# Attention scores by key blocks and residue classes instead of a causal triangle

## The chip, the cores and the metric

The kernel runs on one core of one Trainium2 chip. The metric is the device time of one launch in microseconds (us). A core has five engines that run their own instruction streams side by side and meet through semaphores: PE (TensorE, the matmuls), DVE (VectorE), ACT (ScalarE), POOL (GpSimd) and SP (SyncE, which here only issues DMAs). Matmul results land in PSUM banks; everything else lives in SBUF or in DRAM.

## The reference

One transformer layer, 16 sequences of 512 tokens, width 256, 16 heads of 16, all inputs and outputs fp32:

```
OFFSETS = sorted(set(range(0, 33)) | {48, 64, 96, 128, 192, 256, 384})
scores = jnp.stack([jnp.einsum('bhnd,bhnd->bhn', q, _shift(k, delta, n)) for delta in OFFSETS], axis=-1) * scale
scores = scores + pos_bias.T[None, :, None, :]
alpha = jax.nn.softmax(scores, axis=-1)          # offsets that reach before token 0 are left out
for i, delta in enumerate(OFFSETS):
    out = out + alpha[..., i:i + 1] * _shift(v, delta, n)
gate = jax.nn.sigmoid(x @ Wgate + bgate)
x = layernorm(x + (flat * gate @ Wout + bout))
x = layernorm(x + moe(x))    # router, top 2 of 8 experts, capacity 1024, relu MLP 256 -> 1024 -> 256
```

So a query attends to 40 keys at most: those 0 to 32 tokens back, and seven at 48, 64, 96, 128, 192, 256 and 384 back, all multiples of 16. No other key counts.

## The kernel before

Three stages follow a setup: `attention` (attention, gate, first layer norm, router, scatter of tokens to experts), `experts` and `combine`. Only `setup` and `attention` are touched.

`attention` is a software pipeline over sequences. An iteration `it` has 16 slots, and in each slot every engine does a head part (one of the 16 heads of sequence `it`) and what the table `SLOTS_OF` lists: `proj` (q, k, v, gate projections of the next sequence), `maxp` (a bound for the softmax maximum of the next sequence from the allowed offsets: `near0` to `near3`, `far0`, `far1`, then `t`), `gate`, `outp` and `rout` (output projection, layer norm and router hidden layer of the previous one), `rank` (top 2, expert slots and scatter of the one before that). `split` and `feat` bring in the sequence after next. `AHEAD` says which sequence a stage works on; `LATER` by how many slots an engine comes after PE (1 if not listed). Iterations 2 to 13 are a hardware loop that holds two of them; the others are written out. Each engine runs its stream strictly in this order.

All matmuls are fp16 with a high and a low part, so that three products give nearly fp32. Heads are stacked in pairs on the partitions (e is 0 or 1, 64 partitions each): `qs`, `ks` hold high, low, high parts and in row 49 the negated maximum. For each head:

- PE (`scores`, L519): key-major scores of the causal triangle, four matmuls (512, 384, 256 and 128 queries), 1280 columns in three PSUM banks `st`.
- DVE (`biases`, L804): adds `score_bias`, which holds -1e30 for every offset that isn't allowed, while it moves the scores to `sc`.
- ACT (`weights`, L693, L694): exp twice over 1280 columns, to fp16 (`p16`) and to fp32 (`sc`).
- DVE or POOL (`split_weights`, L384; POOL has 8 of the 16 heads): the low part, fp32 less fp16.
- PE (`values`, L533, L535): 20 matmuls with 128x128 weights into `opv`; ACT (L687) copies pairs of heads to `ob`.

The maximum is found with short matmuls already: near offsets in blocks of 32 queries (L598), far ones by classes of tokens modulo 16 (L615), since all far offsets are multiples of 16. In `rank`, DVE works out the slots (L926 to L947), POOL issues 8 indirect DMAs (L1002) from `y16`, and ACT's next write of `y16` (L761, in `outp` part `y`) waits until they have landed; L887 on DVE makes its low part. `setup` writes `bias_vec`, 128 shifted copies of each head's bias vector, to DRAM, and attention reads it back as `score_bias`.

## Time and profile before

| | us |
|---|---|
| median of 3 runs | 2248.94 (2247.68 to 2251.49) |
| the profiled execution, its own time | 2257.1 |
| its span, first to last instruction | 2255.3 |
| setup, to the first load of attention | 78.85 |
| one iteration of the loop (projection to projection) | 102.0 on average |
| share of the span: DVE, PE, ACT, POOL busy | 71%, 68%, 59%, 40% |

A start in the rows below is in us from the span's start. A PE matmul's duration includes its passage through the array, so a run of short ones is read from start to start. "<-issue" marks idle time in which the engine waited for nothing that the profile shows.

### The profile page before, as it was taken

How to read it: one execution, taken by the hardware profiler on the slowest of the kernel's cores; microseconds unless marked ns; L12 is line 12 of the kernel's file. 1: busy time of each engine (PE TensorE's matmuls, PEld its weight loads, DVE VectorE, ACT ScalarE, POOL GpSimd, SP SyncE). 2: the span in 40 equal slices, each digit the busy share in tenths (PEclk: the TensorE clock that was granted, in tenths of full speed). 3: DMA queues.
4: the chain of work that ended last, by engine and by line, in shares of the span. 5: the costliest groups of instructions: out<-in, count | busy, mean ns of one | idle time of the engine just before them, and what ended most of it. 6: DMA issues, size and time to landing. Idle time of an engine off the chain costs nothing. (4 is left out here: it accounts for less than half of the span.)

```text
span 2255.3 us, 53211 instructions
## 1 busy us (share of the span) xinstructions
PE 1532.9 (68%) x21152; PEld 910.7 (40%) x21152; DVE 1603.1 (71%) x3026; ACT 1333.3 (59%) x1736; POOL 897.9 (40%) x681
## 2 busy tenths in 40 slices
PE   0257778676858677676868586776764499999910
PEld 0134434343434334343434343443432256676710
DVE  4048898887979797977879797979886255555422
ACT  1236776675848576665758585766764366566423
POOL 1223444535454444445354444445353113233242
PEclk9965686776767586776667685867656699999965
DMA  7934331313132230312131321302000334444256
GB/s 108 186 94 141 67 58 50 55 43 62 40 59 51 48 58 32 58 38 52 32 53 47 54 48 34 58 24 48 22 21 12 95 95 85 106 105 88 31 121 196
DMA packets 145705, 150.88 MB, mean 67 GB/s; under 512 B 26287, under 2 KB 134847, under 8 KB 145296
## 3 DMA queue, kind: packets, MB, share of 16 engines
q1 hardware_dynamic: 130112, 132.47, 25.2%
q0 software_dynamic: 15360, 15.10, 4.2%
q8 instruction: 171, 2.80, 0.5%
q14 instruction: 62, 0.51, 0.1%
HBM read 84.70 MB, written 73.70 MB: 70 GB/s over the span
## 5 line engine op out<-in xcount | busy, mean ns | idle before, releaser
L384 POOL TENSOR_TENSOR p<-sc,p 128x1280 f16<-128x1280 f32 x128 | 336.4, 2628 | 536.7 <-ACT sc L694 536.7
L693 ACT ACTIVATE p<-sc 128x1280 f16<-128x1280 f32 x256 | 328.8, 1284 | 360.5 <-PE opv L535 167.6
L804 DVE TENSOR_TENSOR sc<-st,score_bias 128x512 f32<-128x512 f32 (+3 forms) x1024 | 427.5, 478 | 67.4 <-PE st L519 47.1
L694 ACT ACTIVATE sc<-sc 128x1280 f32<-128x1280 f32 x256 | 325.8, 1273 | 0.0
L519 PE MATMUL st<-qs,ks 49*128 49x512 f16 (+3 forms) x1024 | 267.6, 378 | 50.1 <-DVE sc L804 37.2
L384 DVE TENSOR_TENSOR p<-sc,p 128x1280 f16<-128x1280 f32 x128 | 216.0, 1688 | 14.1 <-ACT sc L694 13.2
L533 PE MATMUL opv<-vs,p 128*128 128x33 f16 x2560 | 176.1, 184 | 68.6 <-issue 30.1
L504 PE MATMUL gp<-featT,wr 128*128 128x512 f16 x768 | 204.0, 423 | 1.5 <-ACT featT L708 1.1
L533 PEld LDWEIGHTS opv<-vs,p 128*128 128x128 f16 x2560 | 154.5, 100 | 109.6 <-issue 85.1
L1253 POOL DMA_INDIRECT xln<-y,place x64 | 105.3, 1645 | 220.2 <-DVE y L1395 201.6
L862 DVE TENSOR_REDUCE m_near<-gp 128x8 f16<-128x512 f32 x128 | 82.6, 684 | 148.9 <-remote 92.7
L535 PE MATMUL opv<-vs,p 128*128 128x17 f16 x2560 | 171.8, 175 | 17.1 <-issue 17.1
L1291 PE MATMUL up<-rowsT,w 128*128 128x512 f16 x768 | 173.2, 386 | 9.6 <-DVE w L1368 5.3
L1002 POOL DMA_INDIRECT disp<-y,sidx x128 | 135.2, 1056 | 104.2 <-issue 68.6
L1305 PE MATMUL dn<-w,h 128*128 128x256 f16 x1536 | 170.1, 273 | 0.0
L497 PE MATMUL gp<-ident,x 128*128 128x128 f16 x512 | 53.7, 272 | 170.1 <-ACT x L715 83.9
L1352 ACT ACTIVATE h<-up,b 128x512 f16<-128x512 f32 x128 | 88.1, 688 | 131.1 <-PE up L1291 71.8
L708 ACT COPY featT<-gp 128x1024 f16<-128x1024 f16 x96 | 96.7, 1045 | 111.9 <-PE gp L497 111.6
L535 PEld LDWEIGHTS opv<-vs,p 128*128 128x128 f16 x2560 | 150.7, 100 | 30.0 <-issue 22.2
L1305 PEld LDWEIGHTS dn<-w,h 128*128 128x128 f16 x1536 | 149.7, 98 | 17.3
L519 PEld LDWEIGHTS st<-qs,ks 49*128 49x128 f16 x1024 | 90.2, 108 | 164.5 <-DVE sc L804 79.6
L1407 DVE TENSOR_TENSOR h<-h 128x512 f16<-128x512 f32 x128 | 88.7, 693 | 69.6 <-ACT h L1353 69.6
(158 smaller groups left out, 2956.1 us busy)
## 6 DMA issues: line engine op xcount, KB each, us to landing
qk_dram<-qk SPq DMA_DIRECT2D x64, 256.0 KB, 2.5
qs<-qk_dram SPq DMA_DIRECT2D x96, 128.0 KB, 4.5
ks<-qk_dram SPq DMA_DIRECT2D x96, 128.0 KB, 7.7
disp<-y SPq DMA_DIRECT2D x8, 1040.0 KB, 14.3
rows<-disp SPq DMA_DIRECT2D x16, 520.0 KB, 3.7
xin<-in_L_attn_x SPq DMA_DIRECT2D x16, 512.0 KB, 3.9
xres<-in_L_attn_x SPq DMA_DIRECT2D x16, 512.0 KB
xln<-y SPq DMA_DIRECT2D x16, 512.0 KB, 2.9
```

The lines of the kernel that those rows point to most:

```text
L384: engine.tensor_tensor(p16[:, h % 2, 1, :], sc[:, h % 2, :], p16[:, h % 2, 0, :], ALU.subtract).then_inc(plo_pool if h in POOL_HEADS else ...
L504: last = nc.tensor.matmul(dst, lhs(a, c), rhs(b, c), start=(k == 0), stop=(k == len(todo) - 1))
L519: last = nc.tensor.matmul(st[bank][:, at:at + w], ks[n.par][rows, p, P * j:P * (j + 1)], qs[n.par][rows, p, P * j:N], start=True, stop=True)
L533: nc.tensor.matmul(opv[:, h % 2, i, :], p16[:, h % 2, 0, c:c + P], vs[n.par][:, j, h, :], start=(j == 0), stop=False, skip_group_check=True)
L535: last = nc.tensor.matmul(opv[:, h % 2, i, 0:HD + 1], p16[:, h % 2, 1, c:c + P], vs[n.par][:, j, h, 0:HD + 1], start=False, stop=(j == i), ...
L693: nc.scalar.activation(p16[:, h % 2, 0, :], sc[:, h % 2, :], ACT.Exp)
L694: nc.scalar.activation(sc[:, h % 2, :], sc[:, h % 2, :], ACT.Exp).then_inc(exp_ready, 1)
L804: last = nc.vector.tensor_tensor(sc[:, h % 2, COL[j]:COL[j] + w], st[bank][:, at:at + w], score_bias[:, e, p, 0:w], ALU.add)
L1002: nc.gpsimd.indirect_dma_start(out=disp[:, :], out_offset=bass.IndirectOffsetOnAxis(ap=sidx[:, t, k:k + 1], axis=0), in_=y16[:, t, :].bitc ...
L1253: nc.gpsimd.indirect_dma_start(out=xln[:, :], out_offset=bass.IndirectOffsetOnAxis(ap=place[:, gr, t:t + 1], axis=0), in_=y[:, gr, t, :], ...
L1291: last = nc.tensor.matmul(up[h % 4][:, :], w1[e.par][:, a, c, P * h:P * (h + 1)], rowsT[:, gr, b, c, :], start=(k == 0), stop=(k == 5))
L1305: last = nc.tensor.matmul(dn[u][:, D * (t % 2):D * (t % 2 + 1)], h16[:, gr, a, h, P * t:P * (t + 1)], w2[e.par][:, b, h, :], start=(k == 0 ...
```

## The change

Scores are computed only where offsets can be allowed, in six units ("pairs", since each fills one PSUM bank for each e) for all 16 heads of a sequence, in place of 16 heads. Pairs 0 and 1 are far: tokens of one class modulo 16 against each other, 32x32. Pairs 2 to 5 are near: 64 keys by 32 queries. The bias is added on PE by matmuls of a 0/1 matrix (`sel`) with high and low fp16 parts of the bias (L561, L583), so DVE's pass is gone and ACT reads PSUM. DVE splits bank e = 0 of each pair and POOL bank e = 1. Values need v rearranged in both ways: `vs` goes to DRAM (`v_dram`) and comes back as `v_far` and `v_near`. Far results are evacuated by ACT to `o_far`, written to `o_dram` and read back in token order (`o_back`); DVE adds them to the near results (`merge`, L910). `SLOTS_OF` is arranged anew, and `setup` has no `bias_vec`. A loop iteration has 2496 matmuls instead of 1162: 512 for scores and 1152 for values that are 32 or 64 wide, where 64 and 320 full-width ones stood; 48 more add the bias to the scores; `maxp` keeps its 512 short ones.

```diff
-COL = {0: 0, 1: 512, 3: 896, 2: 1024}
-SCW = 1280
-GP_BANKS, ST_BANKS = 3, 4
+FAR_PAIRS, NEAR_PAIRS = 2, TILES
+GP_BANKS, ST_BANKS = 3, 3
...
+    5: [("outp", "t"), ("rank", "c")],
+    6: [("outp", "w"), ("maxp", "near0"), ("rank", "s0"), ("rank", "s1")],
+    7: [("rank", "s2"), ("rank", "s3"), ("outp", "y"), ("maxp", "near1")], 8: [("maxp", "near2"), ("maxp", "near3")],
+    9: [("maxp", "far0")], 10: [("maxp", "far1"), ("rout", "t"), ("split", "x")],
...
+SCORES_AT = [-1, 0, 4, 7, 10, 12]
+EXP_AT = [0, 1, 5, 8, 11, 13]
+SPLIT_AT = [1, 2, 6, 9, 12, 14]
+VALUES_AT = [2, 4, 7, 10, 13, 15]
+EVAC_AT = [3, 5, 8, 11, 14, 16]
...
+        def split_weights(eng, engine, n, k, e, is_split):
+            eng.wait_ge(exp_ready, n.at(2 * UNIT_PAIRS, 2 * k + e + 1))
+            b = 2 * (k % 2) + e
+            engine.tensor_tensor(p16[:, b, 1, :], p32[:, b, :], p16[:, b, 0, :], ALU.subtract).then_inc(is_split, 1)
...
+                if h == 6:
+                    wait(sp, o_in, n.at(16))
+                    sp.wait_ge(far_out, n.at(FAR_PAIRS, FAR_PAIRS))
+                    for r4 in range(4):
...
+                        sync.dma_start(dst, src).then_inc(o_stored, 16)
+                    wait(sp, merged, n.at(TILES))
+                    sp.wait_ge(o_stored, n.at(64, 64))
+                    sync.dma_start(o_back[:, :, :, :].rearrange("p t h c -> p t (h c)"), o_dram.rearrange("(t p) c -> p t c", p=P)).then_inc(o_in, 16)
...
+            def scores(n, k):
+                if k == 0:
+                    alone.wait_ge(m_in[n.par], n.half(32, 32))
+                wait(alone, exp_ready, n.at(2 * UNIT_PAIRS, 2 * k + 2 - ST_BANKS))
...
+                            for w in range(4):
+                                for e in range(2):
+                                    last = nc.tensor.matmul(banks[e][BLOCK * w:BLOCK * (w + 1), c:c + BLOCK], key[rows[e], 2 * w + z, r:N:FAR_STEP],
+                                                            q[rows[e], 2 * w + z, r:N:FAR_STEP], start=False, stop=(z == 1 and r8 == 7 and w == 3),
...
+                    for b in range(4):
+                        quad = slice(BLOCK * b, BLOCK * (b + 1))
+                        for z in range(4):
+                            for e in range(2):
+                                c = P * z + BLOCK * b
+                                for j, (a, cols) in enumerate(terms3):
+                                    for u in range(2):
+                                        at = (2 * z + e) * OW
+                                        last = nc.tensor.matmul(o[u][quad, at:at + cols.stop - cols.start],
+                                                                p16[halves[u], 2 * (k % 2) + e, a, c:c + BLOCK],
+                                                                v_near[halves[u], 4 * i + b, 2 * z + e, cols],
...
+            def weights(n, k):
+                wait(act, pv_done, n.at(UNIT_PAIRS, k - 1))
+                for e in range(2):
+                    act.wait_ge(st_full[e], n.at(UNIT_PAIRS, k + 1))
+                    bank, b = st[(2 * k + e) % ST_BANKS], 2 * (k % 2) + e
+                    nc.scalar.activation(p16[:, b, 0, :], bank[:, :], ACT.Exp)
+                    nc.scalar.activation(p32[:, b, :], bank[:, :], ACT.Exp).then_inc(exp_ready, 1)
...
-                for vec, copies, src in ((bias_vec, P, vec_b), (near_vec, 32, vec_n), (far_vec, 32, vec_f)):
-                    sp.dma_start(vec, src.unsqueeze(1).to_broadcast([H, copies, vec.shape[2]])).then_inc(stored, 16)
```

DVE before, in the loop, from the residual add of `outp` on: the add and the layer norm's statistics, then a head's bias adds and split, two maximum reductions, another head, and only after `far0`'s reductions the low part of `y16`, which waits for ACT's L761.

```order
L876 SCALAR_TENSOR_TENSOR y<-gp,xres 128x512 [waits xres_ready,gp_full1]
...
L804 TENSOR_TENSOR sc<-st,score_bias 128x512 [waits st_full2,plo_dve]
L804 TENSOR_TENSOR sc<-st,score_bias 128x384 [waits st_full3]
L804 TENSOR_TENSOR sc<-st,score_bias 128x128
...
L866 TENSOR_REDUCE m_far<-gp 128x2x8 [waits gp_full1]
L353 REGISTER_ALU
L866 TENSOR_REDUCE m_far<-gp 128x2x8 [waits gp_full2]
L887 TENSOR_TENSOR y<-y 128x4x256 [waits yh_ready]
```

DVE after, the same stretch: `near0`'s reductions, the first merge, then the low part of `y16` (L992), and behind it the reductions of `near1`, a split, and those of `near2`.

```order
L981 SCALAR_TENSOR_TENSOR y<-gp,xres 128x512 [waits xres_ready,gp_full1]
...
L910 TENSOR_TENSOR ob<-o,o_back 128x136 [waits pv_done]
L910 TENSOR_TENSOR ob<-o,o_back 128x136
L992 TENSOR_TENSOR y<-y 128x4x256 [waits yh_ready]
L368 REGISTER_ALU
L967 TENSOR_REDUCE m_near<-gp 128x8 [waits gp_full1]
L967 TENSOR_REDUCE m_near<-gp 128x8 [waits gp_full2]
L393 REGISTER_ALU
L395 TENSOR_TENSOR p<-p 128x512 [waits exp_ready]
L967 TENSOR_REDUCE m_near<-gp 128x8 [waits gp_full0]
```

What moved: L992 now stands ahead of the reductions that free `gp` banks for `near2`, `near3` and `far0`.

PE after, from the last slot to the first of the next iteration: scores of pair 0, the transposes of `feat`, and scores of pair 1, which need a bank that the exps of pair 0 must have left.

```order
L568 MATMUL st<-qs,ks 32x32 x64
L645 REGISTER_ALU
L130 REGISTER_ALU [waits xh_ready]
L537 MATMUL gp<-ident,x 128x128 [waits gp_drained1]
L537 MATMUL gp<-ident,x 128x128 x7
L537 MATMUL gp<-ident,x 128x128 [waits gp_drained2,xl_ready]
L537 MATMUL gp<-ident,x 128x128 x7
L95 REGISTER_ALU
L561 MATMUL st<-sel,far_bias 128x256 [waits exp_ready]
```

Before, the transposes stood ahead of a head's values and there were four `st` banks.

## Rows read from the trace of the kernel before

**Rows 1.** Windows (stretch, us; PE, PEld, DVE, ACT, POOL busy; granted clock; DMA): iterations 0, 1, 6.

```profile
144.35:218.55 74.20, 51.51 (x961) 28.50 (x961) 53.18 (x96) 50.32 (x59) 30.73 (x17) 0.62 0.53 155
218.55:307.65 89.10, 68.92 (x1085) 39.07 (x1085) 76.84 (x120) 67.52 (x86) 39.07 (x23) 0.73 0.24 49
812.92:917.13 104.21, 74.00 (x1163) 41.81 (x1163) 89.85 (x160) 68.95 (x87) 48.07 (x31) 0.72 0.23 49
```

**Rows 2.** The page, part 5: what the softmax costs off PE.

```profile
L384 POOL TENSOR_TENSOR p<-sc,p 128x1280 f16<-128x1280 f32 x128 | 336.4, 2628 | 536.7 <-ACT sc L694 536.7
L693 ACT ACTIVATE p<-sc 128x1280 f16<-128x1280 f32 x256 | 328.8, 1284 | 360.5 <-PE opv L535 167.6
L804 DVE TENSOR_TENSOR sc<-st,score_bias 128x512 f32<-128x512 f32 (+3 forms) x1024 | 427.5, 478 | 67.4 <-PE st L519 47.1
...
L384 DVE TENSOR_TENSOR p<-sc,p 128x1280 f16<-128x1280 f32 x128 | 216.0, 1688 | 14.1 <-ACT sc L694 13.2
```

**Rows 3.** Groups by form, 800 to 1000 us: two 512-wide reads of PSUM.

```profile
L777 ACT ACTIVATE hid<-gp,br 128x512 f16<-128x512 f32 x15 | 10.9, 728 | 5.5 <-PE gp L504 5.5
L862 DVE TENSOR_REDUCE m_near<-gp 128x8 f16<-128x512 f32 x16 | 10.3, 683 | 18.3 <-remote 16.6 <-PE gp L598 1.6
```

**Rows 4.** Timeline of DVE, POOL and ACT in iteration 6: rank, scatter, layer norm.

```profile
847.66 2.15 DVE L926 TENSOR_SCALAR rdiff<-rexp 128x4 f32<-128x4 f32 x1
853.53 0.16 DVE L947 TENSOR_SCALAR token_id<-token_id 128x4 f32<-128x4 f32 x1
854.71 1.11 POOL L1002 DMA_INDIRECT disp<-y,sidx  x1 [2.62 <-issue]
864.14 0.98 POOL L1002 DMA_INDIRECT disp<-y,sidx  x1 [0.30 <-issue]
870.39 1.28 DVE L876 SCALAR_TENSOR_TENSOR y<-gp,xres 128x512 f32<-128x512 f32 x2
873.92 0.25 POOL L980 TENSOR_SCALAR veps<-mv 128x4 f32<-128x4 f32 x1 [8.80 <-DVE mv L884]
875.83 0.91 POOL L985 TENSOR_TENSOR nmr<-nmr,rstd 128x4 f32<-128x4 f32 x1 [0.18 <-POOL rstd L983]
880.12 1.04 ACT L761 CAST y<-y 128x1024 f16<-128x1024 f32 x1
881.19 1.23 DVE L887 TENSOR_TENSOR y<-y 128x1024 f16<-128x1024 f32 x1 [0.49 <-ACT y L761]
```

**Rows 5.** Timeline of PE: value matmuls, then short ones in one run.

```profile
820.19 0.18 PE L533 MATMUL opv<-vs,p 128*128 128x33 f16 x1 [0.67 <-ACT ob L687]
...
820.24 0.18 PE L533 MATMUL opv<-vs,p 128*128 128x33 f16 x1
...
877.97 1.41 PE L615 MATMUL gp<-ks,qs 16*32 16x32 f16 x128
```

**Rows 6.** PE's instruction packets, MB: whole page, then 1118 to 1122 us; idle times.

```profile
q8 instruction: 171, 2.80, 0.5%
...
q8 instruction: 2, 0.03, 2.9%
...
881.14 0.19 PE L535 MATMUL opv<-vs,p 128*128 128x17 f16 x1 [1.14 <-issue]
1120.95 0.20 PE L533 MATMUL opv<-vs,p 128*128 128x33 f16 x1 [3.65 <-issue]
```

**Rows 7.** Timeline of PE: projections of q and k in iteration 14.

```profile
1532.17 5.28 PE L504 MATMUL gp<-featT,wqk 128*128 128x512 f16 x12 [1.18 <-issue]
1538.60 2.76 PE L504 MATMUL gp<-featT,wqk 128*128 128x512 f16 x12
```

**Rows 8.** Setup: a DMA's KB and us to landing; DVE's last work; PE's first `near0`.

```profile
bias_vec<-og SPq DMA_DIRECT2D x1, 5120.0 KB, 55.0
...
41.19 3.47 DVE L1137 MEMSET ks<- 32x4096 f16 x1 [0.89 <-issue]
...
116.15 0.61 PE L591 MATMUL gp<-near_mask,sel_first 64*128 64x512 f16 x2 [14.17 <-issue]
```

More of the change, by code:

```diff
@@ L187, in run_iterations, with pair_at @@
         one(Batch(None, c))
-def head_at(it, k):
-    n = it.shift(k // H)
-    return (n, k % H) if n.in_range() else None
+def pair_at(it, slot, table):
+    for k, at in enumerate(table):
+        if at % H == slot and it.shift(-(at // H)).in_range():
+            return it.shift(-(at // H)), k
 def tail(rows, dt):
@@ L523, in values @@
[L523 to L536 removed]
+            alone = Apart(pe, pe_passed)
@@ L537, in values @@
                 last.then_inc(pv_done, 1)
             def head(it, k):
[L541 to L543 removed]
+                for what, table in ((values, VALUES_AT), (scores, SCORES_AT)):
+                    if pair_at(it, k, table):
+                        what(*pair_at(it, k, table))
             def feat(n, part):
```

381 lines of the change are left out of this document (221 added, 160 removed), and 9 rows, old and new, of the table SLOTS_OF.

## The prediction

> **What bounds the kernel now.** I read the windows of single iterations first, then the timelines of DVE, POOL, ACT and PE inside one of them. In a loop iteration of 104.2 us DVE works for 89.9, PE for 74.0, ACT for 69.0 and POOL for 48.1 [rows 1]. DVE is within 14 us of full, so it sets the pace, and what feeds it is the softmax: the bias adds (64 a sequence by 478 ns, 30.6 us) and half of the splits (8 by 1.69 us, 13.5 us) [rows 2]. ACT has 32 exps of 1.28 us (41 us), POOL 8 splits of 2.63 us (21 us) [rows 2]. The change takes aim at the right engine; the question is what is late next.
>
> **DVE, ACT and POOL after.** The bias adds are gone. Six pairs leave 6 splits of 512 columns each for DVE and POOL: 512/1280 of 1.69 us is 0.68 us, 4.1 us a sequence, and of 2.63 us 1.05 us, 6.3 us [rows 2]. ACT has 24 exps of 512 columns from PSUM at 0.73 us, 17.5 us [rows 3]. The four merges are two short PSUM reads each, below 0.68 us [rows 3], so 5 us at most; they replace the sum of high and low parts. DVE falls from 90 to about 50 us, ACT to 45, POOL to 33. None of them can bound an iteration any more by its work; by its order, yes (below).
>
> **PE after.** 384 matmuls go, 1712 come. How dear is a short one? Rows of before bound it from both sides. 128 matmuls of 32x32 ran in 1.41 us with 0.24 us of passage in it: 9 ns each [rows 5]. Value matmuls with full-width weights start at 820.19 and, two further, at 820.24: some 26 ns each [rows 5]. The new value matmuls are 32 wide like the cheap ones, but 24 to 48 in a row go to the same 32 columns of the array with only two row halves in turn, where the cheap ones cycle through four column groups. I take 20 ns for values (a pair's 192: 3.8 us) and 10 to 15 ns for scores with their bias matmuls (far pair 2.1 us, near pair 1.2 us).
>
> Instruction supply sets a second floor. PE's queue brought 2.80 MB in 171 packets [rows 6], 16 KB or 128 matmuls with their weight loads. After the loop's branch PE idled 3.65 us and two packets fell into 4 us; after the burst of 128 short ones it idled 1.14 us for no other reason shown [rows 6]. I read this as about 3.1 us a packet once the one in hand is used up: 24 ns a matmul in long runs. An iteration now needs 20 packets, 62 us of its 104, so supply is no bound on average, only inside dense runs, where 20 ns with a packet in hand costs the same. The Trainium skill (Runtime: NRT & Kernel Launch, Instruction fetch mechanics) describes such a fetch, in 16 KiB blocks of 256 instructions, and gives PE an instruction memory of 128 KiB. By that size eight blocks would lie ready and dense runs would not wait, which is rival B below; the idle times in the rows speak against it.
>
> **An iteration after, as a round.** I follow what must be waited for, from the end of pair 2's scores (slot 4).
>
> First leg, off PE. ACT: four exps (2.9 us) [rows 3], two copies of far results and the small exp that `rank` needs (1.0 us, guessed from the small rows of 0.16). DVE: the rank chain, 847.66 to 853.69, 6.0 us [rows 4]. DVE: residual and statistics, 870.39 to 873.92, 3.5 us [rows 4]. POOL: 873.92 to 876.74, 2.8 us [rows 4]. POOL: eight indirect DMAs, 854.71 to 865.12, 10.4 us [rows 4]; they now stand behind that layer norm step. Landing of the last: 2 us (between nothing and the 3 us of other small writes). Then ACT's L869, which waits for it, 1.04 us, and DVE's L992, which waits for L869, 1.23 us [rows 4], and one reduction of `near1`, 0.68 us [rows 3], which frees the bank for `near2`. Ten handoffs at 0.15 us add 1.5. Sum 33.1 us. PE has until then only `outp` t and w, `near0`, values of pair 2, scores of pair 3, `near1`: about 18 us. So PE waits some 14 us here. Before, L761 came at 880.12, 15 us after the last indirect DMA [rows 4], and nobody waited. Behind L869 on ACT stand the exps of pair 3; behind L992 on DVE the reductions and the split of pair 3.
>
> Second leg, PE's own order. `near2` and `near3` at the pace of DVE 4; `far0`, values 3, scores 4, `far1` 10; `rout` and `maxp` transposes with ACT's copy 4; four router steps, two of q, k, two of v and gate. Such a step (12 matmuls of 512) takes 2.6 us at the high granted clock and 5.1 at the low one [rows 7]; I take 2.9, eight are 23.5. Scores 5 and values 4: 5. Values 5, scores 0, `feat`: 7.7. Then a new wait: scores 1 need the first exp pair of pair 0, behind ACT's two `feat` copies, 2.9 us; scores 1, 2.0. Values 0 and 1, the router logits (64 at 26 ns), scores 2: 10.5. Sum 69.6 us. Both legs: 102.7 us. Before, 12 iterations took 1532.17 - 307.65 = 1224.5, 102.0 each [rows 1, 7]. **So the loop gains nothing:** DVE's 40 us are given back to PE and to the scatter chain.
>
> DMA is added too (v out and back twice, far results out and back). v comes back during the projections, which hides it. The far results' trip (store and load, some 8 us) starts at slot 6 and the first merge is wanted on DVE some 14 us after slot 4; it is in time if the stack loads of `qs`, `ks` don't hold it, and even if late by 10 us it ends before L869 does.
>
> **What is surely gained.** Setup waits for `bias_vec`: 5120 KB that take 55 us to land, until attention starts at 78.85 (the table) [rows 8]. Without it the end of setup is DVE's last memset, 44.7 us, plus 3 for more small copies and start-up: -31 us. The first `near0` (116.15) comes a further 3 us sooner, since 4 MB of `score_bias` no longer crowd its loads [rows 8]. Iteration 0 has no scatter, layer norm or router: 74.2 us with DVE at 53 and ACT at 50 [rows 1], by PE's order about 67, -7. Iteration 1 has no scatter: 89.1 to 85, -4. The last iterations without projections: -8. Sum -53.
>
> **Sum.** Loop: 12 x (102.7 - 102.0) = +8. Span 2255.3 - 53 + 8 = 2210. The profiled execution took 2257.1, the median of the runs is 8.2 lower; so 2202 in runs. The legs use durations measured beside a DVE and a POOL that are far busier than they will be; I shorten the round by 0.6 us for that and say **2195 us** (a loop iteration of 102.1).
>
> **Rivals.**
> A, the forecast: iteration 98 to 106.5, 2146 to 2248. Chance 0.45.
> B, short matmuls cost 9 to 12 ns everywhere and supply holds. Values fall from 3.8 to 2 us, five of them on the round: -9 us, and -1.5 from scores. Iteration 92, 2195 - 12 x 10 = 2075. For it: 9 ns in a row. Against: the idle in [rows 6]. Chance 0.23.
> C, slower: each short matmul costs what a full-width one does, 26 to 27 ns [rows 5], and more where supply waits. Values 5.0 us (+6 on the round), scores and `maxp` on the round +6: iteration 114 to 115, 2195 + 12 x 12.5 = 2345. It decides from iteration 106.6 on. For it: same tile in a row, and during the indirect DMAs before, PE is fed slowly too. The Trainium skill (TensorEngine Tiling (Array Packing), Instruction Overhead) puts about 60 cycles on each matmul however small, 25 ns at 2.4 GHz by estimate; the 9 ns of the row contradict it for tiles that alternate, not for these. Chance 0.23.
> D, the far results or v come late, and merges hold DVE and PE beyond the scatter chain: +4 us an iteration, 2245. Chance 0.09.
>
> **Range and chances.** From B's end to short of C's: 2065 to 2330. No change is what a measurement can't tell, within 0.2% (4.5 us). Faster: nearly all of A and B and half of D, 0.68; same 0.05; slower 0.27.
>
> **What would show it.** DVE near 50 us of an iteration; PE busy above 80. PE idle before `near2` some 10 us or more, put down to DVE's reductions, with L869 right after the last indirect DMA's landing. PE idle about 3 us before scores 1 on ACT. Value matmuls 20 ns from start to start, 192 in 3.8 us, with idle by issue in the runs. Setup's end near 48 us. Wrong if values run at 10 ns (then 2075), if PE idles by issue for more than 10 us an iteration beyond today's (then above 2250), or if merges wait for `o_back`.

## The result, and the profile after

The changed kernel takes 2491.99 us (median of 4, 2485.14 to 2502.4), the kernel before 2250.22 beside it: ratio 1.108, 95% interval 1.103 to 1.113. The forecast was 2195 with a range to 2330. The change costs 242 us where I expected a gain of 54.

The page of the changed kernel, engine shares and PE's instruction packets:

```profile
span 2483.5 us, 94541 instructions
PE 1632.6 (66%) x42496; PEld 1076.5 (43%) x42496; DVE 961.5 (39%) x1989; ACT 908.2 (37%) x1544; POOL 648.6 (26%) x654
q8 instruction: 338, 5.54, 0.9%
```

Its windows (columns as in [rows 1]): iterations 0 and 1, then eight loop iterations, from the router logits of one sequence to those eight later.

```profile
116.21:216.37 100.16, 54.44 (x2323) 37.99 (x2315) 24.29 (x36) 23.93 (x47) 16.30 (x15) 0.59 0.54 147
216.37:322.89 106.52, 75.81 (x2427) 49.09 (x2419) 41.99 (x57) 41.72 (x73) 24.24 (x22) 0.68 0.35 73
693.40:1649.50 956.10, 643.93 (x19970) 419.08 (x19969) 363.84 (x712) 331.10 (x593) 251.17 (x233) 0.67 0.32 69
```

The same eight iterations before:

```profile
622.70:1445.20 822.50, 588.53 (x9300) 333.59 (x9300) 694.32 (x1250) 544.06 (x688) 379.45 (x249) 0.70 0.22 47
```

An iteration now takes 119.5 us instead of 102.8. DVE is down from 86.8 to 45.5 us an iteration, ACT from 68.0 to 41.4, POOL from 47.4 to 31.4: what the change aims at is there in full. PE is now the only engine that works more, so I account for its time. Its waits in that stretch (us in total, times, longest), the larger ones:

```profile
PE o L632 <- issue: 68.4, 51, 4.1
PE st L588 <- issue: 46.1, 71, 1.6
PE o L618 <- issue: 45.7, 12, 7.9
PE gp L689 <- DVE m_near L967: 25.4, 16, 2.8
PE st L568 <- issue: 21.7, 16, 2.0
PE gp L537 <- issue: 20.5, 5, 4.8
PE st L561 <- issue: 19.7, 4, 5.6
```

With the small ones, "issue" is 240 us, 30.0 an iteration; before it was 58, 7.3 an iteration. The table below, made the same way for each kernel (windows and PE's waits over eight iterations), is what all that follows is read from. The last three columns add up to the iteration.

| kernel, beside a before of | whole, us | iteration | PE busy | idle by issue | PE waits for others |
|---|---|---|---|---|---|
| before, 2250 | 2250 | 102.8 | 73.6 | 7.3 | 21.6 |
| changed, 2250 | 2492 | 119.5 | 80.5 | 30.0 | 8.9 |
| changed again (c1), 2251 | 2504 | 121.0 | 81.2 | 31.5 | 8.1 |
| changed again (c0), 2147 | 2504 | 121.1 | 79.2 | 24.9 | 16.9 |

So PE is busy 7 us longer, stands 23 us longer for its own instructions, and waits 13 us less for others: +17. Of the 7 us 1.6 are the projection and router steps, whose 512 column matmuls are the same ones but ran at a lower granted clock (0.67 in these iterations against 0.70). In two of the six sets of measurements the kernel before took 2250 us, in the other four 2145 to 2147, by the chip they fell on; the changed kernel took 2492 to 2504 on both kinds of chip. On the first kind idle by issue is larger, on the second the wait for `m_near`. I compare times within one kind; e8, e9 and e10 ran on the first, all other edits on the second.

**What an issue stall is.** PE's timeline of the changed kernel, the values of one pair (192 matmuls) with a stall inside, then an undisturbed pair:

```profile
951.85 1.94 PE L632 MATMUL o<-v_near,p 64*32 64x17 f16 x160 [0.53 <-issue]
956.38 0.60 PE L632 MATMUL o<-v_near,p 64*32 64x17 f16 x32 [2.60 <-issue]
```

```profile
778.12 2.34 PE L632 MATMUL o<-v_near,p 64*32 64x17 f16 x192
```

Undisturbed, 192 take 2.34 us with 0.17 of passage: 11 ns each, near the 9 ns of [rows 5] and not the 20 I took. With a stall inside, the same work takes 5.1 us.

A packet holds 256 instructions, 128 matmuls with their weight loads, so the undisturbed pair has a packet boundary in it too. It cost nothing: a packet had started at 776.66, during the 24 long matmuls before this run, and was there in time. Counting PE's instructions from the loop's branch on shows where the stalls lie. In c0's eight iterations 59 stalls over 0.9 us begin at one and the same place modulo 256, at 7.4 of the 20.5 packet boundaries of an iteration, and PE goes on 1.2 to 1.9 us after a packet has landed. They add up to 20.1 us an iteration; in the first profile they are 56 and 19.2 us. At the other boundaries PE stands for less or not at all. It never gets far ahead: in c0 the packet that started at 1062.15 was the last one for 483 instructions, not quite two packets' worth, and then PE stood.

**How long it lasts depends on the DMA engines.** c0, values of pair 1, and the DMA queues during the stall (packets, MB, share of 16 engines), first part and last part:

```profile
1070.46 1.63 PE L618 MATMUL o<-v_far,p 64*32 64x34 f16 x153
1079.89 0.66 PE L618 MATMUL o<-v_far,p 64*32 64x32 f16 x39 [7.80 <-issue]
```

```profile
q1 hardware_dynamic: 718, 0.65, 115.8%
...
q1 hardware_dynamic: 620, 0.61, 95.7%
q8 instruction: 1, 0.02, 3.4%
```

From 1072.0 to 1076.9 no instruction packet moves, while data fills the engines (the stack loads, and `v_dram<-vs`, which came with the change); PE's packet moves only after 1076.9. Now a stall of c0 with no data on the DMA engines; the only traffic from 1020.9 to 1023.2, which is the packet itself; and the window of the long stall (the last two columns are DMA's share and GB/s):

```profile
1023.25 0.23 PE L632 MATMUL o<-v_near,p 64*32 64x16 f16 x4 [2.06 <-issue]
```

```profile
q8 instruction: 1, 0.02, 3.0%
```

```profile
1072.00:1079.80 7.80, 0.09 (x11) 0.00 (x0) 0.00 (x0) 0.52 (x2) 1.06 (x2) 0.80 1.11 164
```

With no data to pass, a boundary in a dense run costs 2.06 us, with full engines 7.80.

**The off-PE leg**, DVE in c0, then in the run with y stored later (e1, second run):

```profile
967.90 1.25 DVE L967 TENSOR_REDUCE m_near<-gp 128x8 f16<-128x512 f32 x2
978.93 0.50 DVE L910 TENSOR_TENSOR ob<-o,o_back 128x136 f32<-128x136 f32 x2 [9.78 <-DMA o_back<-o_dram]
984.83 1.23 DVE L992 TENSOR_TENSOR y<-y 128x1024 f16<-128x1024 f32 x1 [5.39 <-ACT y L869]
985.97 1.28 DVE L967 TENSOR_REDUCE m_near<-gp 128x8 f16<-128x512 f32 x2
```

```profile
924.82 1.25 DVE L967 TENSOR_REDUCE m_near<-gp 128x8 f16<-128x512 f32 x2
934.83 0.51 DVE L910 TENSOR_TENSOR ob<-o,o_back 128x136 f32<-128x136 f32 x2 [8.76 <-DMA o_back<-o_dram]
935.25 1.28 DVE L967 TENSOR_REDUCE m_near<-gp 128x8 f16<-128x512 f32 x2
```

The reduction that PE needs for `near2` stands behind two waits: the far results' return, then the scatter through L869 and L992. With y later only the first is left. What PE does meanwhile, c0 (from the transposes behind pair 2's scores to `near2`), then the first profile:

```profile
956.14 1.89 PE L537 MATMUL gp<-ident,x 128*128 128x128 f16 x16
...
974.67 0.34 PE L699 MATMUL gp<-ks,qs 16*32 16x64 f16 x20
976.07 0.57 PE L699 MATMUL gp<-ks,qs 16*32 16x64 f16 x44 [1.06 <-issue]
986.71 0.61 PE L689 MATMUL gp<-near_bias,sel 32*128 32x512 f16 x2 [10.07 <-DVE m_near L967]
```

```profile
960.98 0.29 PE L588 MATMUL st<-qs,ks 49*64 49x32 f16 x6 [0.47 <-issue]
961.73 0.25 PE L588 MATMUL st<-qs,ks 49*64 49x32 f16 x3 [0.45 <-issue]
...
970.72 0.60 PE L689 MATMUL gp<-near_bias,sel 32*128 32x512 f16 x2 [2.54 <-DVE m_near L967]
```

On the first kind of chip (the second fence) PE gets a few instructions every 0.7 us while POOL issues its eight indirect DMAs, and so arrives at `near2` when the reduction is nearly ready. On the second it is fed at full pace and waits 10 us instead. The stretch takes the same on both: from pair 2's scores to `near2` 30.2 us in c0 and 30.4 in the first profile, the mean of eight rounds, since the chain ends when it ends. Idle by issue in it is 3.6 and 9.8 us.

### The profile page after: what moved, and what is told of

Its sections match the earlier page's. It is cut to its first block and busy times, and to the rows that moved or that the text cites. A ratio compares the mean times of both kernels' runs of the same rounds, so it can differ in the third digit from the quotient of the medians.

```text
span 2483.5 us, 94541 instructions
## 1 busy us (share of the span) xinstructions
PE 1632.6 (66%) x42496; PEld 1076.5 (43%) x42496; DVE 961.5 (39%) x1989; ACT 908.2 (37%) x1544; POOL 648.6 (26%) x654
## 5 line engine op out<-in xcount | busy, mean ns | idle before, releaser
L395 POOL TENSOR_TENSOR p<-p 128x512 f16<-128x512 f32 x96 | 131.0, 1365 | 794.8 <-ACT p L802 794.8
L395 DVE TENSOR_TENSOR p<-p 128x512 f16<-128x512 f32 x96 | 95.3, 993 | 443.8 <-ACT p L802 443.5
L632 PE MATMUL o<-v_near,p 64*32 64x17 f16 (+1 forms) x12288 | 165.3, 170 | 137.6 <-issue 135.4
L632 PEld LDWEIGHTS o<-v_near,p 64*32 64x32 f16 x12288 | 154.2, 94 | 159.6 <-issue 156.8
L588 PE MATMUL st<-qs,ks 49*64 49x32 f16 (+1 forms) x4096 | 130.6, 207 | 87.2 <-issue 87.0
L801 ACT ACTIVATE p<-st 128x512 f16<-128x512 f32 x192 | 116.7, 608 | 184.6 <-PE st L588 175.7
L544 PEld LDWEIGHTS gp<-featT,wr 128*128 128x128 f16 x768 | 81.6, 111 | 141.4 <-issue 64.6
L588 PEld LDWEIGHTS st<-qs,ks 49*64 49x64 f16 (+1 forms) x4096 | 86.6, 129 | 125.4 <-issue 99.3
L910 DVE TENSOR_TENSOR ob<-o,o_back 128x136 f32<-128x136 f32 x128 | 32.4, 294 | 271.3 <-PE o L632 155.7
L885 ACT ACTIVATE hid<-gp,br 128x512 f16<-128x512 f32 x128 | 89.1, 696 | 122.2 <-PE gp L544 119.8
L802 ACT ACTIVATE p<-st 128x512 f32<-128x512 f32 x192 | 118.0, 615 | 0.0
```

What stands on the lines that cost most here:

```text
L395: engine.tensor_tensor(p16[:, b, 1, :], p32[:, b, :], p16[:, b, 0, :], ALU.subtract).then_inc(is_split, 1)
L544: last = nc.tensor.matmul(dst, lhs(a, c), rhs(b, c), start=(k == 0), stop=(k == len(todo) - 1))
L588: last = nc.tensor.matmul(banks[e][64 * u + first:64 * (u + 1), P * z + BLOCK * b:P * z + BLOCK * (b + 1)], key[rows[e], p, lo - BLOCK + f ...
L632: last = nc.tensor.matmul(o[u][quad, at:at + cols.stop - cols.start], p16[halves[u], 2 * (k % 2) + e, a, c:c + BLOCK], v_near[halves[u], 4 ...
L801: nc.scalar.activation(p16[:, b, 0, :], bank[:, :], ACT.Exp)
L802: nc.scalar.activation(p32[:, b, :], bank[:, :], ACT.Exp).then_inc(exp_ready, 1)
```

## The experiments

Every ratio is to the kernel before on the same chip. The yardsticks are the changed kernel itself, run again on each kind of chip.

**c0_again** and **c1_again**: no edit.

> The changed kernel itself, once more, beside the next three on the same chip, since the first four runs fell on a chip that runs all kernels 4 to 5% faster than the one of the first measurement. Every theory: ratio 1.108 within 0.01. This run is the yardstick for the others of this call, and by its ratio for the earlier ones (there, 1.120 for the later y, 1.116 without the scatter, 1.248 with four terms, 1.103 with two near matmuls). If its ratio is near 1.12, the later y costs nothing and the missing scatter gains nothing.

Measured: 2504.42, ratio 1.166 (1.162 to 1.170). The expected 1.108 missed: the kernel before gains from this chip, the changed one doesn't.

> The changed kernel itself as the yardstick of this call's other three. Every theory: ratio between 1.105 and 1.17, the values seen on two chips; which of them tells nothing by itself. PE's wait before near2 and near3 for the reductions of m_near (L967) was 3 us an iteration in the first profile and 11 in the second, with the longer idle by issue in the first; one of these two patterns should come back.

Measured: 2503.92, ratio 1.111 (1.106 to 1.116), with the pattern of the first profile (3.4 us of `m_near`, 31.5 by issue).

**e1: the store of y back in slot 9.**

```diff
-    7: [("rank", "s2"), ("rank", "s3"), ("outp", "y"), ("maxp", "near1")], 8: ...
-    9: [("maxp", "far0")], 10: ...
+    7: [("rank", "s2"), ("rank", "s3"), ("maxp", "near1")], 8: ...
+    9: [("maxp", "far0"), ("outp", "y")], 10: ...
```

> The changed kernel with one entry of the slot table moved: the store of the layer norm's y goes back from slot 7 to slot 9, where it was before the change. That puts the whole scatter chain (eight indirect DMAs, ACT L869, DVE L992) about 10 us later in an iteration. Theory chain (my first leg and rival C's slowed chain: the end of the round is set off PE): the iteration grows by 5 to 10 us, the kernel by 70 to 140 us. Theory supply (PE waits for its own instructions, the chain is hidden or nearly): within 2 us an iteration, the kernel within 25 us of the changed one, as likely a gain as a loss, because the slow feed of PE beside the indirect DMAs only moves to other matmuls.

> The store of y back in slot 9, once more, as the yardstick of this call. The changed kernel took 2492, 2504 and 2504 us on three chips, though the kernel before took 2250, 2147 and 2251 there; where before took 2250, PE of both kernels gets only about 10 instructions in 0.7 us while POOL runs its eight indirect DMAs, and where it took 2147 it does not, but the changed kernel then waits 11 us for m_near instead of 3. Theory two legs: 2390 to 2420 us where before takes 2147 (as measured), and 2400 to 2450 where it takes 2250, since the slow feed then falls on other short matmuls but the wait is gone. If the gain of 100 us was only a difference of chips: 2490 to 2510 where before takes 2250.

Measured: 2403.54, ratio 1.120 (1.116 to 1.124), then on another chip 2403.02, 1.121 (1.119 to 1.124): 101 us less than c0's 2504. Neither theory expected it the first time; for the second run the range was set from the first. The chain matters, but in the other way: y's steps in slot 7 put L869 and L992 ahead of the reductions, and moving them back takes PE's wait for `m_near` from 12.1 to 3.6 us an iteration. Both runs fell on chips of the second kind, so what it gives on the first was not measured alone.

**e2: no scatter.** One plain DMA in place of eight indirect ones (the waits go from 128 to 16).

```diff
-                    for k in range(2):
-                        nc.gpsimd.indirect_dma_start(out=disp[:, :], ...).then_inc(scattered, 16)
+                    if t == 0:
+                        nc.gpsimd.dma_start(disp[bass.ds(n.at(N), N), :]..., y16[:, :, :]...).then_inc(scattered, 16)
```

> Leaves out the routing's scatter: the eight indirect DMAs of a sequence become one plain DMA on POOL that writes the same 512 token rows once, in token order (the second expert's copy is left out, so the experts get other rows). Everything else of the changed kernel stays. Theory chain: the first leg loses some 9 us of POOL's issue time and the iteration falls by 5 to 9 us, the kernel by 70 to 130 us. Theory supply with a slow feed beside indirect DMAs: the stretch of 10 us in which PE gets about 10 instructions per 0.7 us disappears, which is worth 3 to 6 us an iteration, 45 to 90 us, and the idle by issue at the other packet boundaries (about 3 us each) stays. Theory supply without that special slowness: under 25 us, and PE's idle by issue stays near 30 us an iteration.

Measured: 2398.82, ratio 1.116 (1.113 to 1.120), -106 us, as the chain theory said: iteration 114.6, wait for `m_near` 5.5, idle by issue 25.0, unchanged. It ran on the second kind of chip, so it does not test the slow feed beside the indirect DMAs.

**e3: a fourth term in each value product.**

```diff
-                terms3 = ((0, slice(0, OW)), (0, slice(OW, VW)), (1, slice(0, OW)))
+                terms3 = ((0, slice(0, OW)), (0, slice(OW, VW)), (1, slice(0, OW)), (1, slice(OW, VW)))
```

> Adds to each value product the fourth term (low part of the probabilities by low part of v), 17 columns wide: 384 more short matmuls with their weight loads per sequence, 3 packets of 128, 6144 in all; no other engine gets more work. Theory supply (about 3.3 to 4 us for each packet in a dense run, with PE idle by issue for most of it): +10 to +12 us an iteration, the kernel +150 to +190 us, 25 to 31 ns for each added matmul. Theory tile (a short matmul costs what its own pass through the array takes, 7 to 11 ns in the runs between stalls): +2.7 to +4.2 us an iteration, +45 to +70 us. Theory chain (the end is set off PE): under +25 us.

Measured: 2675.18, ratio 1.248 (1.243 to 1.253), +171 us, 28 ns for each added matmul, as supply theory said and more than the 7 to 11 ns of its own pass. In the iteration's 9.2 us both are there: PE busy +5.7, idle by issue +5.6, waits for others -2.1.

**e4: near values with two matmuls instead of three**, the same columns; DVE adds the two parts.

```diff
-                                for j, (a, cols) in enumerate(terms3):
+                                for j, (a, cols) in enumerate(((0, slice(0, VW)), (1, slice(0, OW)))):
```

> Near values with two matmuls instead of three: the high part of the probabilities by v's low and high part at once (33 columns), then the low part by the high part (17 columns). The same columns go through the array, but 256 matmuls with their weight loads fewer per sequence, two packets of 128; DVE pays for it with two more short adds for each of the four merges (8 a sequence, some 0.3 us each). Theory supply: -6 to -8 us an iteration, the kernel -95 to -125 us. Theory tile by columns: the same number of columns, no change within 20 us. Theory tile by matmul (7 to 11 ns each): -2 to -3 us an iteration, -30 to -45 us. Theory chain: DVE's extra adds count, 0 to +30 us.

Measured: 2368.49, ratio 1.103 (1.099 to 1.106), -136 us, 33 ns for each matmul removed, though the columns are the same. The number of instructions counts, a little more than supply theory said. Of the iteration's 10.1 us, 5.8 are idle by issue and 6.4 PE busy (2.2 of these the projection and router steps, at a granted clock of 0.69 instead of 0.67), less 2.1 of longer waits for others. So 28 and 33 ns are prices of the whole, not of the stalls alone.

**e5: dense runs dealt out between long matmuls** in slots 0, 2, 12 and 13 (values and scores as generators, resumed after each long matmul).

```diff
                     last = nc.tensor.matmul(dst, lhs(a, c), rhs(b, c), start=(k == 0), stop=(k == len(todo) - 1))
+                    if k < len(todo) - 1:
+                        pull(3)
```

> The same instructions on every engine, but PE's program order changes in four slots: the short matmuls of scores 1, values 0, scores 5 and values 4 (576 of them, 4.5 packets of 128, a sequence) no longer stand as dense runs ahead of a projection or router step, but are dealt out between the 512 column matmuls of that step (slots 0, 2, 12, 13), 18 or 24 short ones after each long one. Theory supply (packets of 256 instructions come one at a time, each 3.3 to 4 us after the last, and a dense run uses one up in 1.3 us): the long matmuls (5 to 10 us a step) cover the fetch, -6 to -12 us an iteration, the kernel -85 to -170 us. Theory tile (short matmuls cost what the array takes): nothing or a little worse, within 20 us. Theory chain (end set off PE by the scatter chain): within 20 us, or slower, since scores 1 and 5 and values are complete later.

Measured: 2552.16, ratio 1.190 (1.188 to 1.192), +48 us. Supply and tile theory missed; chain theory had left "or slower" open, but its cause is not the one: the wait for `m_near` stayed at 12.0 us. Idle by issue fell from 24.9 to 21.1 an iteration, but PE's busy time rose from 79.2 to 85.1. The reason is in e15 below.

**e6: interleaving, two near matmuls, router steps one slot later.**

> A version meant to be fast, by theory supply: the interleaving of the run before, near values with two matmuls instead of three (256 matmuls, 2 packets, fewer a sequence), and the four router steps one slot later, so that values 5 and scores 0 (slot 15) also lie between the long matmuls of the last router step. Theory supply: -18 to -28 us an iteration against the changed kernel, the kernel -250 to -390 us, so between 4% slower and 4% faster than the kernel before. Theory tile: -30 to -45 us for the fewer matmuls alone. Theory chain: -30 to +30 us.

Measured: 2440.9, ratio 1.137 (1.135 to 1.140): -63 us against c0, 72 slower than e4 alone. No theory of mine with a gain for interleaving holds.

**e7: long matmuls split in four.**

```diff
-                    last = nc.tensor.matmul(dst, lhs(a, c), rhs(b, c), start=(k == 0), stop=(k == len(todo) - 1))
+                    wide = dst.shape[-1]
+                    step = wide // 4 if wide == 512 else wide
+                    for x in range(0, wide, step):
+                        last = nc.tensor.matmul(dst[:, x:x + step], lhs(a, c), rhs(b, c)[:, x:x + step], ...)
```

> Adds instructions where they are far apart: every 512 column matmul of the projection and router steps becomes four of 128 columns (same columns, same weights loaded four times), 288 more matmuls with their weight loads a sequence, 2.25 packets of 128, 4608 in all. Theory supply, local (a packet costs only where the matmuls between two fetches take less than the fetch): a long step of 12 matmuls takes 5 us and now holds 48, so a fetch of 3.3 to 4 us still fits, 0 to +4 us an iteration, the kernel 0 to +60 us, against about 40 to 50 ns for each matmul added to dense runs. Theory supply, global (each packet costs some 4 us or more wherever it stands): +9 to +13 us an iteration, +130 to +190 us. Theory tile: the added weight loads hide, 0 to +30 us.

The results of the projection and router steps are not complete here. The likely cause is that the four quarters share a PSUM bank and each starts its own sum in it; no run tests that. The instructions are all executed. Measured: 2498.72, ratio 1.164 (1.158 to 1.171): -6 us, less than the 29 us between its own four runs, with 4608 more matmuls and 39 more packets (377). That is supply theory's local form, and tile theory allows it too. Added among long matmuls, instructions cost nothing that shows; added in dense runs, 28 ns each.

**e8 and e9: one eighth of the bytes** of v's and the far results' round trips (e8), of the stack loads (e9), loop only.

```diff
+                            if n.i is not None:
+                                to, src = to[:, 0:1, :], src[:, 0:1, :]
                             sync.dma_start(to, src).then_inc(stack_in[n.par], 16)
```

> Leaves out seven eighths of the bytes of the DMA traffic that the change added, in the loop iterations only: v's store and its four plus four loads, the far results' four stores and their load keep their number, order and waits, but move one eighth (the value products then use old v and old far results). PE's instructions are all there. Theory contention (PE's instruction packets wait behind data on the DMA engines: where DMA is idle a packet boundary costs PE 1.3 us, where the engines are over 90% busy 4 to 7 us): idle by issue falls from 25 to 12 to 18 us an iteration, the kernel by 80 to 170 us against the yardstick. Theory supply by count alone (338 packets at 3.3 us whatever the DMA does): within 20 us. Theory late data (merges and values wait for o_back and v, my rival D): the idle by issue stays and DVE's 7 us an iteration of waits for o_back go, less than 40 us.

> Leaves out seven eighths of the bytes of the stack loads (qs and ks from DRAM, twelve half-stack loads a pair of stages, 1.5 MB a sequence), in the loop iterations only; the kernel before had this traffic too. They run during values 1, where one packet boundary costs 8 us. The scores then use old q and k. Theory contention: the 8 us stall shrinks to 2 to 3, -4 to -7 us an iteration, the kernel -60 to -100 us. Theory supply by count: within 20 us, unless near0's wait for the stack appears in the profile of the yardstick, which it does not.

Measured beside c1's 2503.92: 2471.21, ratio 1.098 (1.093 to 1.103), and 2466.71, ratio 1.093 (1.089 to 1.098): -33 and -37 us, well under what contention theory said. Idle by issue fell from 31.5 to 26.4 and 27.8, the iteration by 2.9 and 3.3. The one long stall that e9 aims at did shrink, from 8 us to under 3; issue stalls in the far values, c1, then e9:

```profile
PE o L618 <- issue: 45.0, 12, 8.1
...
PE o L621 <- issue: 25.3, 12, 2.8
```

e8's time lies inside the range of the late data theory (under 40 us) as well, but that theory left idle by issue as it was, and it fell by 5.1 us an iteration.

**e12: both, with y later.**

> Both reductions of DMA bytes together (leaves out seven eighths of the bytes of v's and the far results' round trips and of the stack loads, in the loop iterations, so old values are used), with the store of y in slot 9. Alone, with y in slot 7, they gave 33 and 37 us. Theory contention with two legs (their gain was cut because the scatter chain then set the end): with the chain out of the way they give -6 to -12 us an iteration against the yardstick, -85 to -165 us. Theory contention as small as measured: -50 to -80 us. Theory supply by count alone: under 30 us.

Measured: 2332.01, ratio 1.088 (1.086 to 1.090), -71 us against e1's 2403: inside the range of contention as small as measured. Idle by issue 25.8 to 19.4. Two stalls that remain:

```profile
939.14 0.23 PE L648 MATMUL o<-v_near,p 64*32 64x16 f16 x4 [3.26 <-issue]
984.40 0.65 PE L634 MATMUL o<-v_far,p 64*32 64x32 f16 x39 [1.74 <-issue]
```

The second is the one that lasts 7.80 in c0. So contention is about 6 of the 26 us of idle by issue in an iteration; the rest stays when seven eighths of this data is gone.

**e10: two near matmuls and y later.** All results complete.

> Near values with two matmuls instead of three (256 fewer a sequence), and the store of y back in slot 9, together; complete results. The first alone took 33 ns for each matmul removed, the second took away a wait of 8 us an iteration before near2 and near3. With the first alone that wait grew to 12.7 us an iteration, so it now hides part of what the fewer packets give. Theory two legs (PE's own order with its packets, and the scatter chain; each gain shows only where its leg ends last): both legs shorten, -16 to -20 us an iteration against the changed kernel, the kernel -225 to -290 us. If each is worth what it was alone: -235. If only one leg counts: -100 to -140.

Measured: 2329.24, ratio 1.032 (1.027 to 1.037), -175 us against c1. All three ranges missed, and it is less than the two parts added (237). Both parts were measured on the second kind of chip; on this one the wait for `m_near` was only 3.4 us to begin with and fell to 2.5, which is the likely reason.

**e11: e6 with y later.**

> The version with interleaved dense runs, near values with two matmuls and router steps one slot later, now with the store of y in slot 9 as well; complete results. Without that move it took 2441 us, with 13.6 us an iteration of waits for m_near before near2 and near3. Theory two legs: most of that wait goes, -9 to -11 us an iteration, 2290 to 2330 us, no better than near values with two matmuls and y later without the interleaving (2329), unless idle by issue, 16 us an iteration there against 27, now counts in full (then 2230 to 2290).

Measured: 2316.76, ratio 1.080 (1.077 to 1.083), -124 us against e6, inside the range. It is 12 us under e10, the same version without the interleaving, but e10 ran on the first kind of chip, where idle by issue is larger. So this pair doesn't show a gain from interleaving.

**e13: one term**, y later.

```diff
+                terms3 = ((0, slice(0, OW)),)
```

> Leaves out the two low terms of all value products (high part of the probabilities by high part of v alone), 768 short matmuls with their weight loads, 6 packets, fewer a sequence, 12288 in all, with the store of y in slot 9; DVE and POOL still make the low parts. Theory supply (28 us of 384 more cost 28 ns each, 256 fewer gave 33 ns each): 28 to 33 ns each, -340 to -405 us against the yardstick, near 2030 us, and so faster than the kernel before wherever that takes 2147 or 2250. Theory tile (9 ns each): -110 us. Theory other leg (a wait off PE takes over once PE is quick): the idle by issue falls by 12 us or more an iteration, but DVE, POOL or DMA waits grow, and the gain stops at 200 to 300 us.

Measured: 2133.27, ratio 0.994 (0.992 to 0.996), -270 us against e1, 22 ns for each matmul. "Another leg takes over" is right: idle by issue falls from 25.8 to 9.0 us an iteration, and DVE and PE now wait like this (eight iterations):

```profile
DVE ob L910 <- DMA o_back<-o_dram: 109.3, 8, 14.8
PE gp L689 <- DVE m_near L967: 90.8, 16, 12.5
```

**e14: as e13, the merge two slots later.**

```diff
-EVAC_AT = [3, 5, 8, 11, 14, 16]
+EVAC_AT = [3, 5, 10, 11, 14, 16]
```

> As the one term version (leaves out the two low terms of all value products, y's store in slot 9), with one more number changed: the merge of the first near pair with the far results (L910, which waits for o_back, the far results' way back from DRAM) moves from slot 8 to slot 10 on DVE, behind the reductions of near1 to near3. In the one term version DVE stood 13 us an iteration at that merge, and PE 11 to 12 us at near2 for the reductions queued behind it. Theory late far results (my rival D, uncovered by the shorter PE leg): PE's wait for m_near falls from 12 to under 3 us, -6 to -10 us an iteration, the kernel -85 to -140 us, near 2020 us. Theory that DVE's merge only waits because nothing else is ready: under 30 us.

Measured: 2048.99, ratio 0.955 (0.952 to 0.958), -84 us against e13, a hair short of the range; the wait for `m_near` went from 12.2 to 3.4 us. The mechanism of my rival D sets the time here once the PE leg is short. This is the fastest kernel of the study, 97 us under the kernel before; it leaves out the two low terms of the value products.

```profile
DVE ob L910 <- DMA o_back<-o_dram: 23.2, 8, 4.1
PE gp L689 <- DVE m_near L967: 19.4, 15, 1.9
```

**e15: as e14, with the interleaving.**

> The run before (one term, y and merge later) with the interleaving of values 0, 4 and 5 and scores 0, 1 and 5 between the long matmuls and the router steps one slot later. Alone, on the changed kernel, interleaving cut the idle by issue by 4 us an iteration and made the kernel 48 us slower, as the scatter chain and the far results' return took the time back; with both out of the way it gave 12 us of 2329 (two near matmuls, y later). Theory supply: the one term version has 9 us an iteration of idle by issue left; interleaving halves it, -3 to -5 us an iteration, -40 to -70 us. Theory that mixing costs PE as much as it saves (PE's busy time rose by 5 to 8 us an iteration with it): within 20 us, or slower.

Measured: 2136.17, ratio 0.995 (0.992 to 0.997), 87 us slower than e14: supply theory missed, the theory that mixing costs more than it saves held. PE busy 76.2 us an iteration instead of 66.2, with the same matmuls. PE's timeline, e14 (not mixed), then e15 (mixed):

```profile
989.72 2.76 PE L544 MATMUL gp<-featT,wr 128*128 128x512 f16 x12 [0.72 <-DVE mT L960]
992.41 0.76 PE L632 MATMUL o<-v_near,p 64*32 64x17 f16 x63
```

```profile
942.13 0.39 PE L544 MATMUL gp<-featT,wr 128*128 128x512 f16 x1
942.45 0.23 PE L648 MATMUL o<-v_near,p 64*32 64x17 f16 x6
942.62 0.39 PE L544 MATMUL gp<-featT,wr 128*128 128x512 f16 x1
942.93 0.23 PE L648 MATMUL o<-v_near,p 64*32 64x17 f16 x6
943.10 0.39 PE L544 MATMUL gp<-featT,wr 128*128 128x512 f16 x1
```

Unmixed, a long one takes (992.41 - 989.72)/12 = 0.22 us and six short ones 0.06: 0.28. Mixed, a round is 943.10 - 942.62 = 0.48. Going from full weights to 64x32 and back costs 0.2 us, some 40 times an iteration here, 8 of the 10 us; in e5, with some 30 rounds, it makes all of the 5.9. Other rounds of e15 take the same (a median of 0.49 over the eight iterations). That is why e5 and e15 lost, and by the same rounds (some 40) most likely e6.

| kernel | iteration | PE busy | idle by issue | waits for others |
|---|---|---|---|---|
| e1 (second) | 113.8 | 79.5 | 25.8 | 8.4 |
| e3 four terms | 130.3 | 84.9 | 30.5 | 14.8 |
| e4 two near | 111.0 | 72.8 | 19.1 | 19.0 |
| e10 two near, y later | 108.8 | 74.3 | 26.8 | 7.5 |
| e12 slim, y later | 106.7 | 77.8 | 19.4 | 9.3 |
| e13 one term | 94.7 | 65.1 | 9.0 | 20.5 |
| e14 merge later | 89.2 | 66.2 | 10.2 | 12.7 |
| e15 interleaved | 95.7 | 76.2 | 11.7 | 7.8 |

## Why the prediction was wrong, step by step

**Where the miss lies.** The first leg, from the end of pair 2's scores to `near2`, was forecast at 33.1 us and takes 30.2 in c0 and 30.4 in the first profile (means of eight rounds). The second leg, PE's own order, was forecast at 69.6 and takes 91.1 and 89.3. So the miss lies in the second, and PE stands idle by issue in it for 21.4 and 20.4 us.

**The step that failed**: "supply is no bound on average, only inside dense runs, where 20 ns with a packet in hand costs the same". The packets are as I counted (338 in all, 20.5 an iteration). But 62 us of 104 is an average that PE can't use: the long matmuls get their own packets in time, yet they don't bank any for the dense runs behind them. The forecast allowed for stalls only in the values: 3.8 us a pair against the 2 of rival B, some 11 us for six pairs. They cost 14.3 there (a pair 4.8 us with its stalls). For stalls in scores, the transposes of `feat` and behind the loop's branch it had no term at all, though [rows 6] shows 3.65 us behind a branch: these are most of the other 15.7 (10.5 in c0, where PE is not fed slowly beside the indirect DMAs). Together idle by issue is 30.0 us an iteration. My own mark, more than 10 us beyond today's means above 2250, was met twice over (22.7).

The Trainium skill (Runtime: NRT & Kernel Launch, Instruction fetch mechanics) gives PE room for 2048 instructions, by which I worked out eight blocks. The traces show a use of that room, but another one. In `experts` of the changed kernel the last pass of the hardware loop, 1340 PE instructions from 2192 to 2279 us, ran without a single instruction packet. In a straight dense run PE stands after less than two packets' worth, and no run shows a reserve of eight. The 7 boundaries of an iteration at which it stands cost 2.7 us each on average.

**Short matmuls**: 11 ns undisturbed, rival B's price. A pair's values take 2.3 us or, with a stall, 5, against my 3.8. Rival C came nearest to the time (iteration 114 to 115, "and more where supply waits", against 119.5) with the wrong price: not 26 ns a matmul. The Trainium skill (TensorEngine Tiling (Array Packing), Instruction Overhead) would have each at 25 ns by estimate; 192 in 2.34 us contradict it.

**Near scores**: I took 1.2 us a pair and left out that their eight bias matmuls alternate with short ones. From one pair of bias matmuls to the next a quarter takes 0.55 us, so a pair 2.2, at the granted clock of 0.50 that this stretch had; in c0 at 1010.9, at 1.00, a quarter takes 0.40, a pair 1.6:

```profile
956.92 0.29 PE L583 MATMUL st<-sel,near_bias 64*128 64x128 f16 x2
957.14 0.40 PE L588 MATMUL st<-qs,ks 49*64 49x32 f16 x16
957.47 0.29 PE L583 MATMUL st<-sel,near_bias 64*128 64x128 f16 x2
```

**Long steps**: I took 2.9 us for each of the eight steps of 12 long matmuls, 23.5 in all. They take 27.6 an iteration, and had taken 26.0 before: the size was too small from the start.

**DVE, ACT, POOL**: forecast 50, 45, 33 us an iteration, measured 45.5, 41.4, 31.4. Right.

**The first leg**: forecast, PE waits some 14 us before `near2`, with L869 right after the scatter. Measured 12.1 on one kind of chip (c0); 4.0 on the other, where PE is fed slowly beside the indirect DMAs and loses the time there. L869 follows the last indirect DMA, as said. The merge waits for `o_back` too, one of my signs of being wrong; in the loop it does end before L869, also as said (978.93 and 983.75 in c0), so only e1 and e14 bring it out.

**The new wait before scores 1**: 2.2 us against 2.9, in four of eight iterations; in the other four the stall behind the branch (4.9 us) stands in its place. Small either way.

**Setup**: the first `near0` comes at 82.30 instead of 116.15 [rows 8], -33.9 against -34. Right. Iterations 0 and 1 were to take 67 and 85 and took 100.2 and 106.5, so -11 became +43. Iteration 0 has no scatter, and there the far results' return alone holds PE for 16 us, which is rival D's mechanism in the changed kernel itself:

```profile
171.25 0.51 DVE L910 TENSOR_TENSOR ob<-o,o_back 128x136 f32<-128x136 f32 x2 [22.81 <-DMA o_back<-o_dram]
172.49 0.61 PE L689 MATMUL gp<-near_bias,sel 32*128 32x512 f16 x2 [16.09 <-DVE m_near L967]
```

Beside it stands idle by issue, 15 us in iteration 0 and 22 in iteration 1.

**Sum**: -34 at the start, +51 up to the first router logits (their start moves from 322.4 to 338.9), +210 over the 15 iterations after, +2 in the rest: the 228 us of the span. The last iterations, forecast 8 us shorter, are 15 longer, inside the +210. e1, e4, e10 and e13 show what can be had back: removing short matmuls from dense runs gives 22 to 33 ns each, and putting y back 101 us on the second kind of chip. Moving the merge gave 84 us in the one term version; in the changed kernel it was not tried.

**Open**: why one kind of chip feeds PE slowly beside indirect DMAs and the other does not. That this also explains 2250 against 2147 for the kernel before is argued only, since no profile of it stands here from the second kind. Whether the fetch waits behind data in a queue or for something else beside it was not separated either; e9 and e12 show only that less data shortens it.

## What to carry to other kernels

When a change trades DVE work for many small matmuls, count instructions per dense run, not per iteration. Here PE stood at a packet boundary, for 2.7 us on average and up to 8, once a dense run had used up what was fetched, at most two packets' worth, whatever the average supply was, and longest where the run fell on a burst of DMA. Fewer instructions with the same columns gave 33 ns each; spreading short ones between full-width ones lost more than it gave. Then look at what stands on the freed engine ahead of the one short step that PE needs: here two waits, each removed by moving one entry of a table, were worth 100 us in the changed kernel and 84 in the one term version.

## What the runs showed of the hardware

- Changing from 128x128 to 64x32 weights and back costs about 0.2 us (a round of 0.48 us instead of 0.28).
- A stall at a packet boundary was 2.06 us with no data on the DMA engines and 7.80 with them full; that second boundary took 1.74 with seven eighths of this data gone.
- A packet boundary costs nothing where its packet came during long matmuls: PE stands for over 0.9 us at about 7 of 20.5 an iteration. A hardware loop of 1340 PE instructions (`experts`) needed no packet in its last pass, while behind each branch of attention's loop two packets come and PE stands for 4.5 to 5.8 us (2.3 to 2.7 with seven eighths of the data gone, e12).
- On one kind of chip PE is fed a few instructions every 0.7 us during POOL's indirect DMAs, on the other it is not: idle by issue in that leg is 9.8 us against 3.6.
- The kernel before runs at a mean granted clock of 0.77 in its runs of 2147 us and 0.74 to 0.75 in those of 2250; the changed kernel runs at 0.71 on both kinds of chip, and in nearly the same time.
